# Node work of a four-layer graph network cut in three parts beside the streams, with the decay layer in half-size slots

## What is computed

```python
# layer 0: two hops
for k in range(2): x = tanh(concat([adj @ x, x]) @ W[k])
# layer 1
out = 1 - 0.1 * x - 0.01 * sum(x * (adj @ x), axis=1)
# layer 2 ("decay"): the last 100 neighbours of each row, the weight halves with each
support = x @ weight; mask = adj != 0; rank = cumsum(mask, 1); deg = rank[:, -1:]
k = minimum(deg, 100); pos = rank - (deg - k)
out = (mask * where(pos > 0, 0.5 ** (k - pos), 0)) @ support + bias
# layer 3, twice (it = 0, 1), with H = adj
Q = x @ Wq + bq;  V = x @ Wv + bv;  edge_feat = H.T @ V                       # "edge"
att = softmax(Q @ edge_feat.T * scale * H, 1).mean(0)                         # "att"
comp_mask = softmax(0.5 * norm(x @ W) + 0.5 * att) >= th_comp
edge_mask = (softmax(cos(x_comp) * H, 1) >= th_edge) & comp_mask[:, None]     # "cos"
agg = (H_pruned.T * dv_isqrt) @ (x_final @ W) * de_inv                        # "down"
x = relu(dv_isqrt * (H_pruned @ agg) @ Theta)                                 # "up"
```

## Time and profile before

| what | value |
|---|---|
| median of three executions | 1884.35 us (1883.01 to 1890.79) |
| profiled execution | 1888.18 us, span 1886.5 us |
| PE, DVE, ACT, POOL busy | 83%, 64%, 36%, 4% of the span |
| granted TensorE clock, mean | 0.939 |
| HBM read | 582 MB, 309 GB/s over the span |
| chain that ended last | PE 47%, DVE 28%, DMA 18% |

### The profile page before, as it was taken

The page is one execution under the profiler, slowest core; times in us unless marked ns, Lnnn a source line. Parts: engine busy times, 40 slices in busy tenths (PEclk is TensorE's granted clock), DMA queues, the critical chain, the costliest instruction groups (busy, mean ns, idle before and its releaser), DMA issues.

```text
span 1886.5 us, 23738 instructions
## 1 busy us (share of the span) xinstructions
PE 1563.6 (83%) x9649; PEld 636.0 (34%) x9670; DVE 1202.5 (64%) x1627; ACT 672.7 (36%) x481; POOL 76.5 (4%) x148
## 2 busy tenths in 40 slices
PE   6789595799799899677768799899996777787895
PEld 2244242333344333222223244443332222232452
DVE  0000202677602688899997899223886999989897
ACT  0000100233201466477760033002664777710341
POOL 0000000233100000000000000000000000000000
PEclk9999899899999999888889999999998888889998
DMA  9959399598579999155549999799993555579994
GB/s 406 426 243 427 131 417 377 178 292 290 217 291 426 390 368 376 64 210 216 215 181 398 426 415 426 299 427 425 377 372 128 186 215 216 190 318 427 425 426 169
DMA packets 60889, 584.99 MB, mean 310 GB/s; under 512 B 6144, under 2 KB 6528, under 8 KB 20608
## 3 DMA queue, kind: packets, MB, share of 16 engines
q1 hardware_dynamic: 60800, 583.71, 77.8%
HBM read 581.99 MB, written 1.70 MB: 309 GB/s over the span
## 4 chain that ended last, share of the span: by engine, by line
PE 47%; DVE 28%; DMA 18%; issue 3%; ACT 2%; POOL 0%; DVEq 0%; SPq 0%; POOLq 0%; ACTq 0%
PE ps L551 46%; DMA slot<-adj_t 10%; DVE pairs L1115 10%; DVE slot L1256 9%; DMA slot<-adj 7%; PE ps L829 1%; DVE slot L1298 1%; DVE slot L1284 1%; DMA x_kept<-cur 1%; ACT pairs L938 1%; DMA pairs<-adj 1%; DVE pairs L1077 0%; DVE negmax L1126 0%; DVE arena L1231 0%; DVE hats L1298 0%
## 5 line engine op out<-in xcount | busy, mean ns | idle before, releaser
L1115 DVE CUSTOM_DVE_ANT_1 pairs<-ps,slot 128x832 f32<-128x832 f32 x352 | 345.6, 1020 | 39.2 <-PE ps L551 20.8
L551 PE MATMUL ps<-hats 64*128 64x416 f32 x832 | 226.0, 651 | 96.7 <-DVE max L1115 94.8
L938 ACT ACTIVATE pairs<-pairs,negmax 128x3327 f32<-128x3327 f32 x88 | 270.1, 3070 | 90.1 <-DVE negmax L1126 90.1
L551 PE MATMUL ps<-slot,cur 128*64 128x512 f32 (+1 forms) x1152 | 218.4, 527 | 28.9 <-DVE slot L1284 20.0
L953 ACT ACTIVATE arena<-pairs,cut 128x3328 fp8e4<-128x3328 f32 x52 | 159.8, 3072 | 88.7 <-DVE cut L1249 88.7
L1256 DVE SCALAR_TENSOR_TENSOR slot<-pairs,cut,slot 128x3327 f32<-128x3327 f32 x52 | 191.1, 3675 | 0.1
L551 PE MATMUL ps<-arena 64*128 64x416 f32 x832 | 164.5, 533 | 3.5 <-DVE max L1115 3.5
L551 PE MATMUL ps<-slot,stat 128*64 128x512 f32 (+1 forms) x672 | 129.9, 538 | 43.7 <-DMA slot<-adj_t 27.9
L551 PEld LDWEIGHTS ps<-hats 64*128 64x128 f32 x832 | 76.8, 214 | 245.2 <-DVE max L1115 190.3
L996 DVE COPY pairs<-ps 128x640 f32<-128x640 f32 x5 | 4.1, 824 | 236.3 <-PE ps L551 236.3
L551 PE MATMUL ps<-pairs,hats 128*64 128x512 bf16 (+3 forms) x1016 | 148.5, 346 | 2.7 <-DVE pairs L1077 2.5
(11 more groups left out here) (170 smaller groups left out, 1547.7 us busy)
## 6 DMA issues: line engine op xcount, KB each, us to landing
slot<-adj SPq DMA_DIRECT2D x173, 1664.0 KB, 9.1
slot<-adj_t SPq DMA_DIRECT2D x70, 1664.0 KB, 15.8
arena<-adj_t SPq DMA_DIRECT2D x28, 1664.0 KB, 22.6
pairs<-adj SPq DMA_DIRECT2D x19, 1664.0 KB, 12.4
slot<-adj_t SPq DMA_DIRECT2D x26, 832.0 KB, 5.0
arena<-adj_t SPq DMA_DIRECT2D x26, 832.0 KB, 5.0
hats<-adj SPq DMA_DIRECT2D x8, 1664.0 KB, 14.8
hats<-adj_t SPq DMA_DIRECT2D x8, 1664.0 KB, 14.0
```

The lines of the kernel that those rows point to most:

```text
L551: return pe.matmul(o, l, r, start=start, stop=stop, skip_group_check=True)
L938: act.activation(bufs[b][:, 0:N], bufs[b][:, 0:N], ACT.Exp, bias=negmax[:, b:b + 1], accum_out=rowsum[:, b:b + 1]).then_inc(exp_done, 1)
L1115: dve.tensor_tensor_reduce(out=pieces3(bufs[k % len(bufs)], c), in0=pieces_psum(piece_place(name, k, c)[0]), in1=pieces3(slot_of(name, k), ...
```

## The change

The node work after `decay1`, after `up0` and after `up1` is cut in three parts of 4, 4 and 5 of the 13 block columns (`CHUNKS`; a part has 8, 8 or 10 of the 26 node blocks). The matmuls are the same; the DVE and ACT instructions on whole tensors become one for each part.

* After `decay0` its half of the sums is complete, and that holds the whole of part 0 (the first 512 of its 832 columns). Part 0 is then worked through during `decay1`: evacuation by ACT at step 1, fold by PE after step 3, bias and centring by DVE at step 4, square by ACT at 5, variance at 6, root at 7, new x at 8, turn by PE after step 10, copy by ACT at 11, value product by PE after 12, value bias by DVE at 14.
* `edge` takes its rows in the order of the parts (`EDGE_ORDER`), so it can start on part 0's rows; its gathers wait for `value_ready` of their part. Parts 1 and 2 are folded after gather 0 of `edge0`, turned after gather 2, and multiplied after gather 4. In `edge1` all but part 2's value product stands ahead of gather 0.
* The other work between gathers moves from k = 1, 5, 9, 13, 16, 19 to k = 9, 11, 13, 16, 18, 21.
* `decay0` and `decay1` load into eight half-size slots in the four `arena` slots. `slot0` to `slot3` are free after `ode`. SP issues the first four loads of `edge0` between the 13th and the 14th load of `decay1`.
* The decay loops are written out. PE reads the support weights directly from `support3`, and the POOL copies are gone.
* The output is stored in three parts.

```diff
+CHUNKS = [slice(0, 4), slice(4, 8), slice(8, HB)]
+EDGE_ORDER = [h * HB + b for c in CHUNKS for h in range(2) for b in range(HB)[c]]
+        half_slots = [early_slots[RING + i // 2][:, i % 2 * HALF:(i % 2 + 1) * HALF] for i in range(EARLY_RING)]
...
+            def decay_stream(q, ks):
+                for k in ks:
+                    n = q * NB + k
+                    free = last_early_use(RING + n // 2) if n < EARLY_RING else BASE["decay0"] + n - EARLY_RING
+                    sp.wait_ge(block_done, EARLY_RING + free + 1)
...
-            stream("decay0", adj_t, 0)
-            stream("decay1", adj_t, 1)
+            decay_stream(0, range(NB))
+            decay_stream(1, range(HB))
+
+            late_stream("edge0", adj, last=RING)
+            decay_stream(1, range(HB, NB))
...
-            pool.wait_ge(support_ready, 1)
-            feed_decay(0)
-            feed_decay(1)
...
+            def fold_part(c, right, ready, value):
+
+                pe.wait_ge(ready, value)
+                for b in range(HB)[CHUNKS[c]]:
+                    last = mm(ps[:, 4 * BANK + b * P:4 * BANK + (b + 1) * P], agg_f[:, b * P:(b + 1) * P], right)
+                last.then_inc(part_folded, 1)
...
+                for k in range(NB):
+                    step(k, last_block=k == NB - 1)
+                    if q == 1 and k == 3:
+                        fold_part(0, ident, agg_cols[0], 1)
+                    elif q == 1 and k == 10:
+                        turn_part(0, 0, cur)
+                    elif q == 1 and k == 12:
+                        value_part(0, 0)
...
-                features_round(4 + it)
-                pe.wait_ge(xt_act, 4 + it)
-                pe.wait_ge(xt_dve, 4 + it)
-                to_nodes(xt, W["value_w"], 0).then_inc(value_psum, 1)
-
-                pe.wait_ge(value_ready, it + 1)
+                if it == 1:
+                    for c in range(3):
+                        fold_part(c, W["theta"], agg_cols[c], 1 if c == 2 else 2)
+                    turn_part(1, 0, cur)
+                    turn_part(1, 1, cur)
+                    value_part(1, 0)
+                    turn_part(1, 2, cur)
+                    value_part(1, 1)
...
+            def decayed_part(c):
+
+                dve.wait_ge(part_folded, c + 1)
+                dve.wait_ge(biased, 1)
+                link(dve.tensor_tensor(of_part(scr_a, c), part_psum(c), of_part(scr_b, c), ALU.add))
+                centre_part(c)
...
+            kept_part(0)
+            kept_part(1)
+            var_part(3, 0)
+            kept_part(2)
+            out_part(0)
+            var_part(4, 1)
+            out_part(1)
+            var_part(5, 2)
+            out_part(2)
```

More of the change, by code:

```diff
@@ L88, in early_places, with last_early_use @@
             order.reverse()
+def last_early_use(slot):
+    order, _ = EARLY_PLACES["ode"]
+    return BASE["ode"] + max(k for k in range(NB) if order[k % EARLY_RING] == slot)
 EARLY_PLACES = early_places()
@@ L95 @@
 KEPT_BLOCKS = RING
-ROW_ORDER = {"edge": list(range(NB)), "att": list(range(NB)), "cos": list(range(NB)),
+CHUNKS = [slice(0, 4), slice(4, 8), slice(8, HB)]
+CHUNK_COLS = [slice(c.start * P, c.stop * P) for c in CHUNKS]
+EDGE_ORDER = [h * HB + b for c in CHUNKS for h in range(2) for b in range(HB)[c]]
+EDGE_CHUNK = [[EDGE_ORDER[k] % HB in range(HB)[c] for c in CHUNKS].index(True) for k in range(NB)]
+ROW_ORDER = {"edge": EDGE_ORDER, "att": list(range(NB)), "cos": list(range(NB)),
              "down": list(range(NB - KEPT_BLOCKS, NB)) + list(range(NB - KEPT_BLOCKS)),
@@ L104, in late_places @@
 def late_places():
-    order, loads = EARLY_PLACES["decay1"]
-    last = {s: BASE["decay1"] + max(k for k in range(NB) if order[k % EARLY_RING] == s) for s in range(RING)}
+    last = {s: last_early_use(s) for s in range(RING)}
     last.update({s: EARLY - 1 for s in range(RING, LATE_SLOTS)})
@@ L272, in build_program @@
         early_loaded = [sem(f"early_loaded{i}") for i in range(EARLY_RING)]
+        half_loaded = [sem(f"half_loaded{i}") for i in range(EARLY_RING)]
         block_done = sem("block_done")
@@ L303, in build_program @@
         proj_read = sem("proj_read")
+        agg_cols = [sem(f"agg_cols{c}") for c in range(3)]
+        part_folded = sem("part_folded")
+        part_centred = sem("part_centred")
+        part_squared = sem("part_squared")
+        part_var = sem("part_var")
+        part_sd = sem("part_sd")
+        part_ready = sem("part_ready")
+        part_turned = sem("part_turned")
+        part_xt = sem("part_xt")
+        part_value = sem("part_value")
         struct_sq = sem("struct_sq")
@@ L362, in place_of @@
         def place_of(name, k):
+            if name.startswith("decay"):
+                n = BASE[name] - BASE["decay0"] + k
+                return half_slots[n % EARLY_RING], half_loaded[n % EARLY_RING], n // EARLY_RING + 1
             if BASE[name] < EARLY:
@@ L438, in stream, with late_stream @@
                         load(ring + k, i)
-            def late_stream(name, source):
+            def decay_stream(q, ks):
[3 more added lines that the diff above has]
+                    sp.wait_ge(block_done, EARLY_RING + free + 1)
+                    dst, loaded, _ = place_of(f"decay{q}", k)
+                    src = halves(adj_t[(NB - 1 - k) * P:(NB - k) * P, :])[:, :, q * QUART:(q + 1) * QUART]
+                    sp.dma_start(halves(dst), src).then_inc(loaded, 16)
+            def late_stream(name, source, first=0, last=NB):
                 kind, it = name[:-1], int(name[-1])
@@ L443, in late_stream @@
                     home, _, free = LATE_PLACES[name, k]
-                    if free is None:
+                    if free is None or not first <= k < last:
                         continue
@@ L696, in _ @@
                     mm(bank(b), zeros_b[:, :], ones_b[:, :])
-                with pe.Fori(0, NB // EARLY_RING) as i:
-                    for k in range(EARLY_RING):
-                        step(k, i)
-                step(NB - 2, 0)
-                step(NB - 1, 0, last_block=True)
-            fold(3, ident, first=0).then_inc(folded, 1)
+                for k in range(NB):
[6 more added lines that the diff above has]
+                        value_part(0, 0)
             def product(name, left, right):
@@ L863, in _ @@
                     up_gather(2 * pair + 1)
-                fold(5 + 2 * it, W["theta"]).then_inc(folded, 1)
+            for c in range(3):
+                fold_part(c, W["theta"], agg_cols[c], 2 if c == 2 else 3)
         @block.scalar
@@ new lines, in value_part, with relu_part @@
+            def value_part(it, c):
+                dve.wait_ge(part_value, 3 * it + c + 1)
+                bias = per_feature4(value_bias)[:, :, CHUNKS[c]]
+                dve.tensor_tensor(of_part(scr_a, c), part_psum(c), bias, ALU.add).then_inc(value_ready, 1)
+            def relu_part(n, c, dst):
+                dve.wait_ge(part_folded, n + 1)
+                for h in range(2):
+                    new = dve.scalar_tensor_tensor(out=of_part(dst, c)[:, h], in0=part_psum(c)[:, h], scalar=0.0,
+                                                   in1=part_spread(small["dv"][:, :], c)[:, h], op0=ALU.max,
+                                                   op1=ALU.mult)
+                return new
```

259 lines of the change are left out of this document (165 added, 94 removed).

## The result

The changed kernel takes 1862.08 us (median of four executions, 1859.59 to 1863.25), the kernel before beside it 1885.01: a ratio of 0.987 [0.985, 0.990], 22.9 us less. The forecast was 1858.9 us, 3.2 us lower than what came.

A forecast was written before the change was run, and what follows sets the result against it. No engine bounds the whole: PE fills `decay0`, PE and DMA nearly fill `edge0`, PE and DVE alternate between. 21.0 - 3.2 + 6.7 + 2.0 = 26.5 us, rounded to 25.5, gives 1858.9 us from 1884.35; range 1850 to 1869, whole 1848 to 1874.

The forecast's parts named there:

- Part 1: Node work of the first part inside `decay1`: adds 3.2 us on PE's path, with DVE's pieces causing no stall.
- Part 2: Loads in `decay1`: block 13 lands at 459.5 us behind four full loads, 1.8 us to spare, no stall.
- starved case: Rival, chance 0.11: the four full loads in `decay1` don't overlap, PE stops 10.6 us, total 1869.5 us.
- edge stream at 358 GB/s: Rival, chance 0.04: `edge0` turns DMA-bound at 4.76 us per load, total 1873 us.
- Part 3: From the last decay matmul through `edge0` to `att0`: 106.4 us instead of 127.4, 21.0 us less.
- 6 us of pure wait: Ahead of `att0`: what the store of x cost before, now hidden by the longer tail of PE work.
- Part 4: From `up0` to the end of `edge1`: 107.0 us instead of 113.7, 6.7 us less, bounds 4.5 to 8.
- Then 73.3 + 18.5 + value part 2 1.2 + 4.3 wait = 97.3: PE's time in `edge1` from gather 0: gathers, other products, last value product and the wait for `hat`, in us.
- Part 5: The end after `up1`: 2.5 us earlier relu, 2 us lost to DVE instructions, 1.2 us shorter store; gain 2.0 us.
- Slower: code loading: Rival, chance 0.04: eight more code pieces in the written-out decay stop PE 5.7 us each, 45.6 us, total 1904 us.

The follow-up runs named there:

- e6: Changed kernel with no node work in `decay1`, all three parts behind the last decay matmul: 1873.1 us, ratio 0.993 to the kernel before.
- e2: Changed kernel with the first four loads of `edge0` behind all loads of `decay1`: 1863.3 us, ratio 0.989 to the kernel before.
- e9: Changed kernel with the decay passes in eight full-size slots again and the four early `edge0` loads behind the last decay load: 1865.4 us, ratio 0.989.
- e4: Kernel before, with DVE instead of SP waiting for the store of x ahead of the `att0` loads: 1880.7 us, ratio 0.997.
- e10: Kernel before with only the names of the four slot tiles turned by two places: 1884.9 us, ratio 0.999.
- e12: Kernel before with 40 useless matmuls added on PE, where it waits for DVE ahead of `edge0`: 1880.2 us, ratio 0.997.
- e1: Changed kernel with the `hyper_w` product and two query halves two gathers earlier, the turn of `hat` unmoved: 1856.3 us, ratio 0.984 to the kernel before.
- e7: Changed kernel with `edge1` alone taking turns, value products and other work in the old order: 1858.0 us, ratio 0.985 to the kernel before.
- e11: Changed kernel with the names of the four slot tiles turned by two places: 1864.6 us, ratio 0.990 to the kernel before.

## Why the prediction was right, and where its terms were off

Means over the profiles of each form (three of the old, ten of the new, or those in which the stretch isn't edited) add up to the measured difference: `decay` +3.4, D to att0 -19.4, att0 to up0 -1.3, up0 to att1 -1.3, att1 to up1 -3.4, end -0.9: -22.9 us, and 22.9 were measured. That they agree to the tenth is chance, since the interval of the ratio allows 19.6 to 28.7 us. The forecast was 25.5. Point by point:

* *Part 1, +3.2 us.* Measured +3.4. No wait of PE in `decay1` is over 0.33 us. e6, which has the written-out loops and no copies on POOL but no node work there, takes 152.7 us: both are worth 0.3 us at most.
* *Part 2, block 13 at 459.5 us with 1.8 us to spare.* It landed at 457.5, its mask started at 459.9: 2.4 us. The starved case and the edge stream at 358 GB/s are out: the windows show 421 GB/s in `edge0`. What the prediction didn't ask is whether the early loads are needed, and e2 and e9 show that they aren't.
* *Part 3, D to att0 106.4 us.* Measured 108.2. The wait for the turn of `hat` was 4.28 us (4.3 foretold), the waits at the turns 0.9 (1.1). The failed term is what follows the wait: I counted the five products at 3.06 us each, and the turn took 4.73 at half clock. That is 1.7 of the 1.8 us. The store of x is hidden, as said, but with 0.7 us to spare and not 3.5, and it had cost 3.1 us before (e4), not "6 us of pure wait". It took 11.3 us to land behind two loads, where I took 7.2 + 2.0, and it was issued 2 us later than reckoned.
* *Part 4, -6.7 us.* This is the term that failed: -4.0 between the first two profiles and -1.3 between means. Two causes. The first profile of before was long here: gather 0 came 17.2 us after `up0`, and 15.7 in e4, e10 and e12, and the stretch is 113.1 to 113.5 us in those three. The 6.8 us at a clock of 0.50 that only the first profile has (shown under e4) are the difference. The prediction saw the low clock there (0.79) and gave it up to 2 us in its bounds, but took the whole 113.7 us as the kernel's own. So some 3 us of gain were never there to be had: against those three profiles the changed form, 113.0 us in the mean, gained 0.3 us here. The second cause is the step "Then 73.3 + 18.5 + value part 2 1.2 + 4.3 wait = 97.3". Gather 0 came at 9.1 us (9.7 taken), but the gathers took 100.6 us: 1.7 for the half clock behind the wait, 1.0 for the load at 1205.25, the rest in small pieces. In the four profiles with 6.8 us at half clock they took 101.4 to 101.9 us. e1 and e7 shorten or remove the wait and get 5 to 6 us back.
* *Part 5, -2.0 us.* Measured -0.9. Its own terms, 2.5 - 2 + 1.2, give 1.7. The relu came 2.4 us earlier as reckoned. The instructions that parts add cost DVE all of it, not 2 us of it, and the last store gave back 0.9 instead of 1.2.
* *Not in the sum at all:* -4.7 us in the stretches without an edit. For the 3.4 us of att1 to up1 e12 supports a cause, the place of the pieces of code within the pass. The 1.3 us of att0 to up0 aren't clear of scatter: ten profiles of changed forms lie between 554.9 and 560.1 us, and the first cos pass differs between the two profiles of the changed kernel itself (202.5 and 200.4 us). The rival "Slower: code loading" had the queue right and the direction wrong. Five more pieces came, 72 instead of 67 in the page's row of that queue, where it counted eight; no stop of PE went with them, and the pieces in the second cos pass stand at a place that gained.

So the sum was near by luck as well: an unforeseen gain of 4.7 us covered most of the 8.1 us by which parts 3 to 5 fell short. The mechanism that carries the result is the one foretold, node work of part 0 before D, which also lets the other two parts stand between gathers. e6 prices the two together at 10 to 11 us net. It leaves 5 of the 19.4 us. Beside the profile of the kernel before, e6 starts gather 0 8.5 us earlier after D, takes 6.1 us longer from there to the last gather (the wait for `hat` and the low clock are in it), and starts `att0` 2.5 us sooner after the last gather, where the store's wait was.

## What to carry to other kernels

Take the sequential work of one part of a stage into the pass before it, even if that pass is full: 3 us there bought 14 us at the border. When other work is moved between steps of a stream, measure each DVE chain that it starts against the steps up to its use, since a wait of some 4 us cost more than itself here through the clock. Before a difference of two profiles is explained, profile a second build of each form: here one stretch was off by 3 us because one execution had a low clock in it, and another was 3 us shorter in every profile of the changed form though nothing in it was edited. And look at the granted clock of the stretch that is to gain, in more than one profile, before its low clock is counted as a gain.

## What the runs showed of the hardware

* PE's idle stretch of 4.1 to 4.3 us ahead of the turn of `hat` stands 15 times in the profiles of changed forms, and each time the granted clock fell to 0.50 (1.2 GHz) at its end or right behind it: for 3.4 us ten times, for 6.8 us five times. The turn then took 4.3 to 4.7 us or 5.4 to 5.8 us instead of 3.06. Behind the nine idle stretches of 1.5 us ahead of the same turn (e7 and the old forms) the turn ran at the full clock.
* The same waits don't always bring the same clock: behind `up0` one profile of four of the old form has 6.8 us at 0.50, which cost some 3 us, and the others have none.
* A 16 KB piece of code that comes while a 1.7 MB load is under way can delay it: the load above took 7.99 us, the one issued at 1572.38, without a piece, 6.6; the counts over all profiles stand under e10 and e11. Where DVE has no slack, a wait of 0.8 to 1.4 us follows. The Trainium skill, "Runtime: NRT & Kernel Launch", section Instruction fetch mechanics, says that code comes in 16 KiB blocks of 256 instructions and that crossing a block is mostly hidden. The traces agree for PE, whose longest wait in the written-out `decay1` is 0.33 us, and show that DVE can pay the price when it waits for data.
* So the number of PE instructions ahead of a stage can move its time: in the one build tried, 40 matmuls that compute nothing made the kernel before 6.4 us faster [3.8, 9.1].
